# A decoder layer on one core: the 64-step recurrence and the 71 expert tiles written out without loops, the expert's first layer computed transposed from weights copied ahead

## The reference, cut to what matters

```
x = x + attn(layernorm(x))                 # 16 heads of 8, one shared k and v
x = x + xattn(layernorm(x), ctx, ...)      # 64 steps:
    h0, c0 = lstm(concat(x_t, a), h0, c0)
    h1, c1 = lstm(h0, h1, c1)
    attn = softmax(einsum('bh,bsh->bs', h1 @ Wq.T, ctx))
    a = tanh(concat(attn @ ctx, h1) @ Wo.T + bo)      # a is also the output
x = x + ffn(layernorm(x), ...)             # 8 experts, D = 128, FF = 512, top 1:
    h = relu(x @ W1[e] + b1[e]); y = h @ W2[e] + b2[e]; out = gate * y
```

## Time and profile before

| | us |
|---|---|
| median of 3 runs | 1651.74 (1650.35 to 1654.31) |
| the profiled execution, its own time | 1653.54 |
| its span, first to last instruction | 1651.8 |
| granted TensorE clock over the span, share of full | 0.935 |
| PE busy | 1395.1 (84%) |
| PE weight loads busy | 1215.9 (74%) |
| DVE busy | 1139.0 (69%) |
| ACT busy | 737.2 (45%) |
| POOL busy | 430.7 (26%) |
| recurrence, about | 490 to 1440 |
| expert tiles, about | 1443 to 1652 |

### The profile page before, as it was taken

How to read it: one execution, slowest core, us unless ns; L and a number is a source line. 1 busy time by engine, 2 the same in 40 slices (tenths; PEclk the granted TensorE clock), 3 DMA queues, 4 the chain that set the end, 5 groups by cost and what they waited for, 6 DMA issues and landing times. The chain is left out here.

```text
span 1651.8 us, 86284 instructions
## 1 busy us (share of the span) xinstructions
PE 1395.1 (84%) x34396; PEld 1215.9 (74%) x34397; DVE 1139.0 (69%) x4573; ACT 737.2 (45%) x2083; POOL 430.7 (26%) x1194
## 2 busy tenths in 40 slices
PE   1627777777558999999999999999999999499997
PEld 1426666666437998888888888888888889366665
DVE  5879888888674677666776666666676666545454
ACT  2427777777523444444444444444444444133332
POOL 0000000000010233333333333333333333323333
PEclk9759998999858999999999999999999999689999
DMA  7000000000144000000000000000000000122221
GB/s 242 1 1 1 0 0 0 0 0 0 43 118 132 13 18 16 14 14 11 14 14 13 14 14 14 14 14 11 14 14 13 14 15 16 45 85 76 72 72 42
DMA packets 42140, 50.64 MB, mean 31 GB/s; under 512 B 5674, under 2 KB 33836, under 8 KB 41800
## 3 DMA queue, kind: packets, MB, share of 16 engines
q1 hardware_dynamic: 35376, 34.98, 7.3%
q0 software_dynamic: 5376, 12.66, 2.2%
q10 hardware_dynamic: 1304, 1.86, 0.3%
HBM read 30.52 MB, written 19.48 MB: 30 GB/s over the span
## 5 line engine op out<-in xcount | busy, mean ns | idle before, releaser
L452 POOL TENSOR_TENSOR X<-X,yv 128x128 f32 (+1 forms) x64 | 29.4, 459 | 412.4 <-DVE yv L662 412.4
L1059 PE MATMUL sc_ab<-h_a,KH 128*128 128x48 f16 (+2 forms) x4096 | 124.5, 183 | 5.1 <-issue 2.2
L1059 PE MATMUL sc_ab<-h_b,KH 128*128 128x48 f16 (+2 forms) x4096 | 123.7, 183 | 0.0
L1059 PEld LDWEIGHTS sc_ab<-h_a,KH 128*128 128x128 f16 x4096 | 113.5, 96 | 9.7 <-DVE h_a L1396 2.3
L986 PE MATMUL z_a<-h_a,WL 128*128 128x64 f16 x2304 | 113.2, 194 | 7.6 <-DVE h_a L1388 1.9
L1109 PEld LDWEIGHTS mx_ab<-pmv_b,VH 128*128 128x128 f16 x4096 | 107.0, 96 | 16.3 <-DVE pmv_b L1439 16.3
L1109 PE MATMUL mx_ab<-pmv_b,VH 128*128 128x16 f16 x4096 | 112.9, 169 | 5.3 <-DVE pmv_b L1439 0.4
L986 PE MATMUL z_b<-h_b,WL 128*128 128x64 f16 x2304 | 112.4, 194 | 5.1 <-DVE h_b L1388 0.4
L1132 ACT ACTIVATE gt_a<-z_a,sc 128x256 f32<-128x256 f32 x128 | 60.6, 474 | 121.1 <-PE z_a L986 121.1
L1059 PEld LDWEIGHTS sc_ab<-h_b,KH 128*128 128x128 f16 x4096 | 113.9, 96 | 0.0
L1109 PEld LDWEIGHTS mx_ab<-pmv_a,VH 128*128 128x128 f16 x4096 | 112.0, 97 | 2.1 <-issue 1.1
(11 more groups left out here) (297 smaller groups left out, 3756.5 us busy)
## 6 DMA issues: line engine op xcount, KB each, us to landing
xr<-sorted_x SPq DMA_DIRECT2D x72, 129.0 KB, 2.1
XT<-in_ctxT SPq DMA_DIRECT2D x1, 4096.0 KB, 13.5
x_scratch<-X SPq DMA_DIRECT2D x1, 4096.0 KB, 16.1
x1r<-x_scratch SPq DMA_DIRECT2D x64, 64.0 KB, 1.8
X<-in_w SPq DMA_DIRECT2D x1, 2048.0 KB, 9.1
b_sb<-in_b SPq DMA_DIRECT2D x1, 2048.0 KB, 22.8
sorted_x<-zt SPq DMA_DIRECT2D x12, 129.0 KB, 9.5
out<-ys,xr POOLq DMA_INDIRECT x72, 2.3
```

The source lines that it names most:

```text
L452: nc.gpsimd.tensor_tensor(xrow, xrow, yv[:, 1 - u, :, :].rearrange("p (g a) d -> p a g d", g=4), ALU.add).then_inc(g_x1, 1)
L1059: mm = nc.tensor.matmul(A.S[:, WIDE * n:WIDE * n + streamed(n)], KH[:, k, pair * P:(pair + 1) * P], A.h[1][:, 2 * n:2 * n + streamed(n) // ...
```

## The change

1. `run_steps` of the recurrence writes out all steps 0 to 67; `turn` has no effect there.
2. `run_tiles` writes out all tiles; NT is 71 (64 + 8 - 1, which is enough for any split of 8192 tokens over 8 experts).
3. The first layer is computed transposed: hidden(j) takes four blocks of 128 columns of W1 as stationary operand and xgT as moving one, so that psHa (three blocks) and psHv (the fourth) hold h transposed, and no transposition follows. The stationary blocks are read from `w1_e`, two buffers into which DVE copies the expert's [128, 512] of W1 two tiles ahead (`weights`).
4. b1 then lies along partitions: `b1_sb` is [128, 32], passed from the host as `b1T`, and is the bias column of the ReLU: ACT does three blocks (ACTIVATE with bias), DVE the fourth (add, max).
5. `etab` holds the expert's number alone; the columns are computed in registers. PE, ACT and DVE each read it once per tile.

```diff
-NT = B * T // P + NE
+NT = B * T // P + NE - 1
...
         def run_steps(eng, first_half, step, turn):
             first_half()
-            for t in range(HEAD):
-                step(t, t % SLOTS)
-            with nc.Fori(HEAD, T - TAIL - turn + 1, turn, engines=[eng.engine], hint_back_edge=True) as t:
-                for k in range(turn):
-                    step(t + k, (HEAD + k) % SLOTS)
-            for t in range(T - TAIL, T + 4):
+            for t in range(T + 4):
                 step(t, t % SLOTS)
...
-                    sync.dma_start(b1_sb[:, :], b1.rearrange("(a e) f -> a (e f)", a=1).broadcast_to([P, NE * FF])).then_inc(d_w, 16)
+                    sync.dma_start(b1_sb[:, :], b1T).then_inc(d_w, 16)
...
-                        step(nc.vector.tensor_scalar(tex[:, :], tex[:, :], float(NE - 1), None, ALU.min))
-                        step(nc.vector.tensor_scalar(etab[:, 0, :], tex[:, :], float(FF), None, ALU.mult))
-                        step(nc.vector.tensor_scalar(etab[:, 1, :], tex[:, :], float(D), None, ALU.mult))
+                        step(nc.vector.tensor_scalar(etab[:, :], tex[:, :], float(NE - 1), None, ALU.min))
...
             def run_tiles(eng, step):
-                head = RING + 6
-                for j in range(head):
-                    step(j, j % RING)
-                body = (NT - 2 - head) // RING * RING
-                with eng.Fori(head, head + body - RING + 1, RING) as j:
-                    for k in range(RING):
-                        step(j + k, (head + k) % RING)
-                for j in range(head + body, NT + 1):
-                    step(j, j % RING)
+                for j in range(NT + 1):
+                    step(j, j % RING, j == 0)
...
-                    def hidden(j, u, col):
+                    def hidden(j, u):
                         pe.wait_ge(a_xt, j + 1)
-                        wait(pe, v_hb, j - 1)
-                        nc.tensor.matmul(psH[:, u, :], xgT[:, u, :], w1_sb[:, bass.ds(col, FF)],
-                                         start=True, stop=True).then_inc(p_h, 1)
-
-                    def turn_hidden(j, u):
-                        pe.wait_ge(v_hb, j + 1)
+                        pe.wait_ge(v_w1, j + 1)
                         wait(pe, a_ht, j - 1)
+                        wait(pe, v_ht, j - 1)
                         for c in range(FC):
-                            mm = nc.tensor.transpose(psHT[:, u, c * P:(c + 1) * P], hb[:, u, c * P:(c + 1) * P], ident[:, :])
-                        mm.then_inc(p_ht, 1)
+                            h = psHa[:, u, c * P:(c + 1) * P] if c < FC - 1 else psHv[:, u, 0:P]
+                            mm = nc.tensor.matmul(h, w1_e[:, u, c * P:(c + 1) * P], xgT[:, u, :], start=True, stop=True)
+                            if c == FC - 2:
+                                mm.then_inc(p_ha, 1)
+                        mm.then_inc(p_hv, 1)
...
-                    def relu(j, u):
-                        act.wait_ge(p_ht, j + 1)
+                    def relu(j, u, e):
+                        act.wait_ge(p_ha, j + 1)
                         wait(act, p_y, j - 1)
-                        nc.scalar.activation(hT[:, u, :, :].rearrange("p c n -> p (c n)"), psHT[:, u, :],
-                                             ACT.Relu).then_inc(a_ht, 1)
+                        for c in range(FC - 1):
+                            ins = nc.scalar.activation(hT[:, u, c, :], psHa[:, u, c * P:(c + 1) * P], ACT.Relu,
+                                                       bias=b1_sb[:, bass.ds(e * FC + c, 1)])
+                        ins.then_inc(a_ht, 1)
...
+                    def weights(j, u, e):
+                        wait(dve, p_hv, j - 1)
+                        nc.vector.tensor_copy(w1_e[:, u, :], w1_sb[:, bass.ds(e * FF, FF)]).then_inc(v_w1, 1)
+
+                    def relu(j, u, e):
+                        c = FC - 1
+                        dve.wait_ge(p_hv, j + 1)
+                        wait(dve, p_y, j - 1)
+                        nc.vector.tensor_scalar(hT[:, u, c, :], psHv[:, u, 0:P], b1_sb[:, bass.ds(e * FC + c, 1)], 0.0,
+                                                ALU.add, ALU.max).then_inc(v_ht, 1)
...
+                        if tile(j + 2):
+                            of[(k + 2) % RING] = expert(dve, j + 2)
+                            weights(j + 2, u, of[(k + 2) % RING])
                         if tile(j + 1):
-                            add_b1(j + 1, 1 - u)
+                            relu(j + 1, 1 - u, of[(k + 1) % RING])
                         if tile(j - 1):
-                            add_b2(j - 1, 1 - u)
+                            add_b2(j - 1, 1 - u, of[(k - 1) % RING])
                             finish(j - 1, (u8 + RING - 1) % RING)
```

More of the change, by code:

```diff
@@ L1515, in decoder_kernel @@
             psX = ps("psX5", [P, 2, 512])
-            psH = ps("psH", [P, 2, 512])
-            psHT = ps("psHT", [P, 2, 512])
+            psHa = ps("psHa", [P, 2, 512])
+            psHv = ps("psHv", [P, 2, 512])
             psY = ps("psY", [P, 2, 512])
@@ L1616, in _, with step @@
                     turn(0, 0)
-                    hidden(0, 0, first_column(0))
                     turn(1, 1)
-                    def step(j, u8):
+                    hidden(0, 0)
+                    def step(j, u8, fresh):
                         u = u8 % 2
-                        if tile(j + 1):
-                            next_col = first_column(j + 1)
-                        if tile(j - 1):
-                            before_col = first_column(j - 1)
                         if tile(j + 2):
                             turn(j + 2, (u8 + 2) % RING)
-                        if tile(j):
-                            turn_hidden(j, u)
                         if tile(j + 1):
-                            hidden(j + 1, 1 - u, next_col)
+                            hidden(j + 1, 1 - u)
                         if tile(j - 1):
-                            output(j - 1, 1 - u, before_col)
+                            output(j - 1, 1 - u, expert(pe, j - 1))
                     run_tiles(pe, step)
@@ L1680, in _, with tile_step @@
                     dve.wait_ge(s_wf, 16)
-                    add_b1(0, 0)
-                    def tile_step(j, u8):
-                        u = u8 % 2
+                    of = {0: expert(dve, 0), 1: expert(dve, 1)}
+                    weights(0, 0, of[0])
+                    weights(1, 1, of[1])
+                    relu(0, 0, of[0])
+                    def tile_step(j, u8, fresh):
+                        u = u8 % 2
+                        k = u8
+                        if fresh and not (isinstance(j, int) and j == 0):
+                            of[(k - 1) % RING] = expert(dve, j - 1)
+                            if tile(j):
+                                of[k] = expert(dve, j)
+                            if tile(j + 1):
+                                of[(k + 1) % RING] = expert(dve, j + 1)
+                        if tile(j + 2):
+                            of[(k + 2) % RING] = expert(dve, j + 2)
+                            weights(j + 2, u, of[(k + 2) % RING])
                         if tile(j + 1):
-                            add_b1(j + 1, 1 - u)
+                            relu(j + 1, 1 - u, of[(k + 1) % RING])
                         if tile(j - 1):
-                            add_b2(j - 1, 1 - u)
+                            add_b2(j - 1, 1 - u, of[(k - 1) % RING])
                             finish(j - 1, (u8 + RING - 1) % RING)
```

55 lines of the change are left out of this document (27 added, 28 removed).

## The result

| | before | after |
|---|---|---|
| median of 4 runs, us | 1651.05 (1648.71 to 1654.31) | 1587.22 (1586.23 to 1589.20) |
| span of the profiled execution, us | 1651.8 | 1584.9 |
| granted clock over the span | 0.935 | 0.939 |

The ratio is 0.9614, 95% interval 0.9594 to 0.9633: the changed kernel is faster, with a median of 1587 us against the 1591 that stands above. The medians are 63.8 us apart, the two profiled executions 66.9.

What follows compares the result with a forecast made beforehand. Recurrence (TensorE nearly never idle, plus loop cost) and expert tiles (TensorE's queue part of the bound) were taken to bound the kernel. 23.8 + 0.4 + 36.5 = 60.7 us off 1653.54 gives 1592.8, 1591 as median; range 1575 to 1609.

Steps and rivals of the forecast that it cites:

- The whole, 60.7: Whole kernel: sum of the gains forecast for recurrence, tables and expert tiles, 60.7 us off the profiled execution.
- The recurrence, 23.8: Recurrence without a loop: 52 steps from 14.28 to 13.90 us and step 60 from 17.94 to 13.90, together 23.8 us.
- The 4.0 of step 60: Recurrence, where all engines leave their loops: step 60 goes from 17.94 to 13.90 us, 4.0 us saved.
- the upper bound: Recurrence: of bounds 4.0 (only the exit goes) and 24 us (every step like the written-out ones), the latter was taken.
- The tables and the start, 0.4: Expert table, before the last barrier: two of three operations on DVE go, 0.20 us each, 0.4 saved; first psY unmoved.
- The expert tiles, 36.5: Expert tile stage: 71 tiles at 2.15 us each, 149.9 us against 186.4 before, 36.5 us saved.
- the ring: Expert tiles: the next weight copy waits on DVE behind ReLU and bias add; 4.3 us for two tiles, 2.15 each.
- TensorE alone, 2.00: Expert tiles: TensorE's own work per tile, 0.14 + 0.89 + 0.97 = 2.00 us.
- TensorE bound: Rival, expert tiles: handovers overlap and tiles take 1.97 us, 12.6 us less, 1578 us; chance 0.22.
- The input row loads run eight tiles ahead and cost nothing at this pace.: Expert tiles: loading the input rows was forecast to add no time at the forecast tile pace.
- Instructions too late: Rival, recurrence: TensorE runs dry once in every written-out step, 17.94 us each, 210 us more, 1801 us; chance 0.03.
- The sign: Whole kernel: faster with chance 0.96, slower 0.03, within 0.2% of no change 0.01.

Runs made afterwards that it cites:

- tiles_flat_old: Kernel before with only the expert tiles written out, in their old form, the recurrence still looping: 1642.17 us, ratio to before 0.9931.
- rec_only: Kernel before with only the recurrence's steps written out, the expert tiles keeping their loops and old form: 1630.05 us, ratio to before 0.9867.
- deep_only: Changed kernel with 12 instead of 8 slots of xr for the input rows and nothing else: 1587.92 us, ratio to before 0.9603.
- load_early: Changed kernel where VectorE reads the table entry for tile j+3 behind the weight copy for tile j+2, not ahead of it: 1581.25 us, ratio to before 0.9573.
- w_three: Changed kernel with three buffers of w1_e instead of two, VectorE copying the weights of tile j+3: 1586.12 us, ratio to before 0.9594.
- deep_w_three: Changed kernel with three buffers of w1_e and 12 instead of 8 slots of xr: 1572.69 us, ratio to before 0.9523.

## Why the prediction was right

**The whole, 60.7.** The sum is nearer than its terms. Between the two profiled executions steps 1 to 63 gave 22.7 where 23.8 stood, the stretch from there to the first psY gave -0.9 where 0.4 stood, and the tiles gave 39.0 where 36.5 stood. The errors of -1.1, -1.3 and +2.5 cancel, which is luck. The other 6.0 of the 66.8 us (3.7 up to step 0, 2.3 in step 0) were not forecast. tiles_flat_old, whose code is that of before up to there, reaches step 0 1.4 us earlier (496.72) and takes 2.3 us less for it (15.08), so at least 3.7 of the 6.0 are the spread of executions and not the change. The 1.8 taken off for the median allowed for a part of it.

**The recurrence, 23.8.** Measured 22.7 in the trace between steps 1 and 63, and 20.7 by rec_only's median. The 4.0 of step 60 came in full, but the prediction named only the hole of 2.19 us for it; the other half is the granted clock of 0.81, which it did not mention, and which went with the hole. The steps went to 13.92, not 13.90: five of them are 0.1 to 0.3 longer. The choice of the upper bound, argued from the written-out steps at both ends, was right.

**The tables and the start, 0.4.** The first psX came 44.73 after step 63 instead of 45.09. That looks like the 0.4 of the term, but rec_only, which keeps the three table operations, has 44.56, and all runs lie between 43.9 and 46.1, so no run shows the term. The first psY came 11.34 after psX instead of 10.04. What TensorE waited for in it is new:

```profile
1417.10 0.48 PE L1581 MATMUL psX<-ident,xr 128*128 128x128 f32 x1 [12.46 <-DMA xr<-sorted_x]
...
1423.05 1.62 PE L1590 MATMUL psHa<-xgT,w_e 128*128 128x128 f32 x6 [4.33 <-DVE w_e L1649]
```

(PE's timeline of the changed kernel.) VectorE waits for the load of b2 before its first table read, so even the first product now waits for b2; before, psH did not. That the change made the stretch longer isn't shown, though: with the old form of the tile it took 11.89 in rec_only and 11.82 in tiles_flat_old, at a granted clock of 0.50, against 0.59 in the profiled execution of before, and with the new form 10.7 to 11.7. The weights need no b2, and that wait could stand behind the two copies; no run has it there.

**The expert tiles, 36.5.** Measured 39.0, at 2.12 a tile for the 2.15 of the sum: 2.1 us of the 2.5 over 70 intervals. The links, forecast and measured: psY to ReLU 0.25 and 0.24; ReLU to bias add 0.35 and 0.26, since the add starts before the ReLU's recorded end; to ys 0.36 and 0.32; to the copy 0.77 and 0.75; copy 0.43 and 0.43; to hidden 0.15 and 0.10; hidden and output 2.0 and 2.19. The 0.77 was read from a row in which the add also waited for psY, whose end at 1642.65 lies 0.29 before the add's start, so that row gave no more than an upper bound; that 0.75 came out is partly luck. The instance above closes at 4.29, the stage's mean is 4.24. deep_only, load_early and w_three show that it is the ring: slots alone change nothing, and either cut of the ring gives tiles of 1.90. The copy took 0.427 here too. The Trainium skill (VectorE: DVE Perf Modes, The TRN2 errata) gives the formula by which it would be 0.33, and says in the same section that this formula comes out too low and that the measured fixed term is about 150 cycles; with that the estimate is 0.42, and the trace agrees.

**TensorE alone, 2.00.** Too high: it needs 1.90 (17 passes 0.1115 apart). The rival "TensorE bound" had its price too small for that reason: 70 intervals of 1.90 instead of 2.15 are 17.5 us, not 12.6. That the ring closes faster than TensorE's own work did not come true in this kernel; load_early is what that rival would look like.

**"The input row loads run eight tiles ahead and cost nothing at this pace."** This was right for this kernel, as deep_only shows, and the words "at this pace" carried it: at 1.90 a tile they cost 12.7 us between the psY in w_three and 2.4 in the profiled execution of load_early.

**Instructions too late.** TensorE never ran dry in the 64 written-out steps: the instruction packets on the page rose from 55 to 229, the steps stayed at 13.92, and between steps 1 and 63 TensorE has no idle stretch above 1 us. That agrees with what the Trainium skill says of sequential prefetch (Runtime: NRT & Kernel Launch, Instruction fetch mechanics), down to its blocks of 16 KiB, 16,384 B here. What it cost in w_three was on the side of the other transfers.

**The sign** rested on written-out steps and tiles in the same trace, and no run came near turning it.

## What to carry to other kernels

When a kernel holds a looped and a written-out form of the same step, read both: here the written-out one forecast the unrolled stage to 0.2% in the recurrence (13.90 against 13.92) and to 2% in the tiles (2.42 against 2.46 in tiles_flat_old). A new form of the work and unrolling can need each other to pay: here the parts gave 12 and 14 us alone and 39 together. When an engine stands still for 2 us, read the granted clock behind it too; in step 60 it cost as much as the hole. Before cutting a ring, ask what runs at nearly its pace: a ring's cut that gives nothing by the median may only have uncovered the next one, and the two edits together gave 14.5 us where one alone gave 1. When a sum comes out right, compare its terms as well.

## What the hardware showed that was not expected

- In w_three a 16,384 B packet of instructions took one DMA engine for 0.9 to 1.5 us, every 10 to 13 us of written-out tiles, and the last packets of a 129 KB load came about a microsecond late beside it. With 8 buffers, which come round every 15 us at 1.90 us a tile, that was 12.7 us between the psY (w_three against deep_w_three); with 12 it was nothing. In the profiled execution of load_early, with the same packets and 8 buffers, it was 2.4 us.
- Leaving a loop cost about as much on several engines at once as on one: 3.3 us with only TensorE's loop, 4.6 with only the others', 4.0 with all, over a step of 13.90. In tiles_flat_old, with other code behind the recurrence, it was 6.4. Of each, 1.2 to 2.2 us are matmuls at the lower level of the granted clock (0.81 to 0.90 over the step), the rest is idle time.
- The clock can fall without an idle stretch: in step 41 of tiles_flat_old it was 0.89, the step took 15.68 us instead of 14.32, and TensorE has no gap above 0.2 us there or in the 3 us before.
- A looped step cost 0.14 us through the engines with four steps a turn and 0.26 through TensorE with one step a turn.
